# Two attention layers with heads of 16: projections ahead of the values, other banks for them, and a new order on ScalarE and VectorE

## The chip, the cores and the metric

The kernel runs on one core of a Trainium2 chip. Its engines are TensorE (PE; its weight loads are listed as PEld), VectorE (DVE), ScalarE (ACT), GpSimd (POOL) and SyncE (SP, which only issues transfers). The metric is the device time of one launch in microseconds; lower is better.

## The reference

The input x is 32 sequences of 64 tokens with 256 features, and ctx a second tensor of that shape. Four layers follow each other:

```python
x = L0(x, ctx, ctx)         # two cross attentions with 16 heads of 128, each behind a layer norm, and an MLP
x = L1(ctx, x, mask1)       # keys and values from concat(ctx, x): 128 keys, 16 heads of 16; norm, MLP
x = L2(x, ctx, mask2)       # layer norm, keys and values from ctx: 64 keys, 16 heads of 16; norm, MLP
x = L3(x, ctx)              # a 32-channel non-local block with a batch norm
```

The change touches L1 and L2, in their attention:

```python
q = (x_in @ q_w + q_b).reshape(B, Q, 16, 16)
k = (keys_in @ k_w + k_b).reshape(B, T, 16, 16);  v = (keys_in @ v_w + v_b).reshape(B, T, 16, 16)
weights = softmax(mask(einsum('bqhd,bthd->bhqt', q, k) * scale))
out = einsum('bhqt,bthd->bqhd', weights, v).reshape(B, Q, 256) @ out_w + out_b + residual
```

Q is 64; T is 128 in L1 and 64 in L2. All is computed in fp32; matrix products with weights run as three products of split operands (a high part rounded to the fast format, and the rest, the low part).

## The kernel before

`narrow` (L1215) builds both layers; `own` is true for layer 1. A layer is NU turns: 32 of one sequence in layer 1, 16 of two sequences in layer 2. NH = 8 half chunks of 256 tokens are projected, one for 4 turns in layer 1 (a group) and one for 2 in layer 2. A turn u covers all 16 heads, so its probabilities are 128 rows by 1024. Each engine has its program written out by hand, with semaphores between them:

- **TensorE** (`pe`, L1453): scores of u (`pe_scores`, L1410 for the mask and L1417), values of u - 3 (`pe_values`, L1447), the uses of banks of turn u (`pe_use`), transposes of u - 2 (`pe_transpose`, L1432).
- **ScalarE** (`act`, L1529): high part of the values of u - 3 (`act_hi`, L1579), the first use, the exponential (L1542), other uses whose bank the transposes need, the copy of the transposed probabilities of u - 2 (`act_probs`, L1565), the rest, and the normalised tiles of the next norm (L458).
- **VectorE** (`dve`, L1628): maximum (L1643) and subtraction (L1647) of u, low part of the values of u - 3 (`dve_lo`, L1618), its uses (`dve_use`: output unit L1612, bias row L1608), parts of a norm (statistics L384 and L409, rsqrt steps L433 to L442, a low half L488), sum (L1623) and reciprocal (L1626) of u - 1.
- **GpSimd** (`pool`, L1730): copies of keys (L1710), bias rows (L345), splits of weights (L1693, L1697), the power in a norm (L499), and the multiplication by the reciprocal (`pool_normalise`, L1755) of u - 1.

A use of a bank is a unit of matmuls that fills one of the 8 banks of the accumulator, and its eviction. Kinds: `q`, `kc`, `kh` (queries, keys from ctx, keys from x; evicted by ScalarE in L1503 and L1521), `v` (values; L1515), `norm` (transposes of a norm, L519; evicted by ScalarE in L533, with a high part in L537), `out` (output projection) and `row` (the bias row), both evicted by VectorE. `Slots.put` lists the uses of each turn in order, `bank_for` gives each its bank, and the unit waits until the use before it in that bank has been evicted. The projections all go through the helper `split3` (L175).

Banks: scores 0 to 3; transposes BT = 4 and 5; values BP = 6 in layer 1, 5 and 6 in layer 2; uses BJ, which share a bank with the transposes. A unit in bank 4 or 5 waits for the copy of the transposes that stood there, and the transposes wait for its eviction. In layer 2 the second half of the transposes (bank 5) also waits for the low part of the values that stood there (L1429).

## Time and profile before

| | |
|---|---|
| median of 3 runs | 1619.66 us (1619.57 to 1622.58) |
| the profiled execution | 1622.66 us |
| its span | 1621.1 us |
| TensorE busy | 1534.3 us, 95% |
| VectorE, ScalarE, GpSimd busy | 976.7, 861.7, 389.2 us |
| granted TensorE clock, mean | 0.993 |
| layer 1's attention | about 1038 to 1205 us |
| layer 2's attention | about 1311 to 1427 us |

The profile is of one execution. The span is from the first to the last instruction. Starts are counted from the start of the span; a line is that of the kernel, and for operations through a helper that of the helper. Engines overlap, so busy times do not add up to the span. A bracket behind a row tells how long its engine had been idle, and whose end released it.

### The profile page before, as it was taken

The numbers are of one execution on the slowest core, as the hardware profiler recorded it, in microseconds if no ns is written. First come the engines' busy times: TensorE is split into PE (matmuls) and PEld (weight loads), VectorE is DVE, ScalarE is ACT, GpSimd is POOL, SyncE is SP. The second block draws the span as 40 slices with busy tenths as digits, with TensorE's granted clock in tenths as the row PEclk, the third lists the DMA queues.
The fourth block names the chain that finished last, engine by engine and source line by source line (L and its number), as shares of the span: only waits on it lengthen the run. The fifth ranks groups of instructions, "written<-read, shape, count | busy, mean of one in ns | idle before, by whom it ended". The sixth has DMA issues, their size and how long they took to land. (4 is left out here: it accounts for less than half of the span.)

```text
span 1621.1 us, 43103 instructions
## 1 busy us (share of the span) xinstructions
PE 1534.3 (95%) x18156; PEld 1352.6 (83%) x18156; DVE 976.7 (60%) x2019; ACT 861.7 (53%) x1623; POOL 389.2 (24%) x365
## 2 busy tenths in 40 slices
PE   8999999999999999999999999888889987899995
PEld 6989888899888989988889889777778876788863
DVE  7755555555686555555555673588875565764366
ACT  5544444444455444444444555666776565665475
POOL 1211011101233110110111140166561133431042
PEclk9999999999999999999999999999999999999998
DMA  5111010000001101010100000200010000000001
GB/s 202 34 34 34 2 34 34 17 19 34 34 2 34 34 1 34 34 34 2 34 28 4 25 27 1 79 2 2 28 54 27 1 28 28 3 2 27 14 15 52
DMA packets 18701, 46.13 MB, mean 28 GB/s; under 512 B 1456, under 2 KB 11712, under 8 KB 15440
## 3 DMA queue, kind: packets, MB, share of 16 engines
q1 hardware_dynamic: 14320, 39.17, 7.1%
q10 hardware_dynamic: 4192, 4.24, 0.8%
q8 instruction: 144, 2.36, 0.6%
q14 instruction: 45, 0.37, 0.1%
HBM read 39.21 MB, written 4.19 MB: 27 GB/s over the span
## 5 line engine op out<-in xcount | busy, mean ns | idle before, releaser
L175 PE MATMUL ps<-ch,W 128*128 128x512 f32 (+1 forms) x2592 | 595.8, 377 | 4.5 <-DVE W L243 2.9
L175 PEld LDWEIGHTS ps<-ch,W 128*128 128x128 f32 x2592 | 439.4, 188 | 85.5 <-DVE W L243 3.2
L175 PEld LDWEIGHTS ps<-W,split_arena 128*128 128x128 f32 x3084 | 392.9, 189 | 41.3 <-issue 7.0
L175 PE MATMUL ps<-W,split_arena 128*128 128x256 f32 x3084 | 409.3, 284 | 16.5 <-DVE split_arena L1047 7.4
L175 PE MATMUL ps<-W,ch 128*128 128x256 f32 x1632 | 223.8, 287 | 0.0
L175 PEld LDWEIGHTS ps<-W,ch 128*128 128x128 f32 x1632 | 203.8, 191 | 1.0 <-ACT arena L776 0.2
L742 ACT ACTIVATE arena<-ps 64x256 f32<-64x256 f32 x256 | 97.0, 379 | 193.2 <-PE ps L655 190.1
L833 DVE TENSOR_REDUCE small<-ps 128x4 f32<-128x260 f32 x128 | 54.0, 422 | 204.0 <-PE ps L617 204.0
L791 ACT ACTIVATE arena<-ps,hbias 128x512 f32<-128x512 f32 x128 | 88.1, 688 | 126.7 <-PE ps L175 126.7
L210 POOL TENSOR_TENSOR arena<-arena 128x256 f32<-128x256 f32 x16 | 11.9, 742 | 588.0 <-PE ps L175 586.4
L916 DVE TENSOR_TENSOR arena<-ps,arena 128x512 f32<-128x512 f32 x128 | 88.0, 691 | 106.8 <-PE ps L175 105.6
L1047 DVE TENSOR_TENSOR split_arena<-arena,split_arena 128x512 fp32r<-128x512 f32 x96 | 70.2, 731 | 130.7 <-ACT split_arena L1079 121.6
L1755 POOL TENSOR_TENSOR arena<-arena,small 128x1024 f32<-128x1024 f32 x48 | 91.8, 1914 | 174.8 <-DVE small L1626 174.8
L765 ACT ACTIVATE arena<-arena 128x260 f32<-128x260 f32 x128 | 54.4, 425 | 139.5 <-DVE arena L836 139.5
L1076 ACT ACTIVATE arena<-ps,cols 128x512 f32<-128x512 f32 x96 | 66.0, 688 | 99.0 <-PE ps L175 97.3
L826 DVE SCALAR_TENSOR_TENSOR split_arena<-ps,hbias,split_arena 128x256 fp32r<-128x256 f32 x256 | 105.6, 474 | 1.5 <-ACT split_arena L749 1.5
L856 DVE TENSOR_TENSOR x_sb<-ps,x_sb 128x512 f32<-128x512 f32 x128 | 87.5, 687 | 18.2 <-PE ps L175 18.1
L749 ACT ACTIVATE split_arena<-ps,hbias 128x512 fp32r<-128x512 f32 x128 | 81.0, 684 | 26.1 <-PE ps L668 26.1
L668 PEld LDWEIGHTS ps<-arena 64*64 64x64 f32 x4096 | 65.5, 134 | 22.3 <-issue 21.8
L776 ACT ACTIVATE arena<-ps,hbias 128x512 f32<-128x512 f32 x128 | 80.1, 676 | 2.8 <-PE ps L175 2.8
L1643 DVE TENSOR_REDUCE small<-ps 128x8 f32<-128x1024 f32 (+1 forms) x48 | 58.2, 1212 | 34.7 <-PE ps L1417 34.2
L499 POOL TENSOR_TENSOR small<-small 128x4 f32<-128x4 f32 x24 | 26.5, 1103 | 218.2 <-DVE small L418 201.6
(135 smaller groups left out, 1972.5 us busy)
## 6 DMA issues: line engine op xcount, KB each, us to landing
raw<-wpack SPq DMA_DIRECT2D x23, 1028.0 KB, 5.0
arena<-vb_in SPq DMA_DIRECT2D x16, 256.0 KB, 5.1
x_sb<-x_in SPq DMA_DIRECT2D x4, 512.0 KB, 8.2
arena<-ctxT SPq DMA_DIRECT2D x4, 512.0 KB, 9.1
spill<-x_sb ACTq DMA_DIRECT2D x1, 2048.0 KB, 8.8
arena<-spill ACTq DMA_DIRECT2D x1, 2048.0 KB, 8.3
arena<-ctx_tok SPq DMA_DIRECT2D x16, 128.0 KB, 2.1
out<-x_sb SPq DMA_DIRECT2D x7, 256.0 KB, 2.5
```

Source lines behind the costliest of these rows:

```text
L175: last = e.matmul(dst, lhs[a], rhs[b], start=start and n == 0, stop=stop and n == 2, skip_group_check=True)
L668: ins = e.matmul(ps[dims, BO + b, at:at + SEQ], vs[t % 2][keys, n, h * DH0 + d * SEQ:h * DH0 + (d + 1) * SEQ], pts[h][keys, n, :], start=T ...
L742: ins = e.activation(pts[h][b * SEQ:(b + 1) * SEQ], own[:, :, b * SEQ:(b + 1) * SEQ], ACT.Copy)
L749: e.activation(head_split(h, 0), head_cells(h), ACT.Identity, bias=head_col(t, 3, h)).then_inc(a_oh, 1)
L776: e.activation(ks[h][:, :, key_slots(h)], cut(ps[:, h, :], BPC), ACT.Identity, bias=head_col(u, 1, h)).then_inc(a_ke, 1)
L791: e.activation(qs[h], ps[:, 2 + h, :], ACT.Identity, bias=head_col(u, 0, h)).then_inc(a_qe, 1)
L826: ins = e.scalar_tensor_tensor(head_split(h, 1)[:, :, b, :], head_cells(h)[:, :, b, :], head_col(t, 3, h), head_split(h, 0)[:, :, b, :].bi ...
L856: e.tensor_tensor(xs, cut(ps[:, banks[j], :], 2), xs, ALU.add).then_inc(a_acc, 1)
L916: e.tensor_tensor(vs[u % 2][:, 2 * j:2 * j + 2, :], cut(ps[:, j, :], 2), each(vdiff[u // NCH % 2], 2), ALU.add).then_inc(a_ve, 1)
L1047: e.tensor_tensor(gsp[f % 2][1], gelu[:, f % 2, :], gsp[f % 2][0].bitcast(F32), ALU.subtract).then_inc(s["gl"].sem, 1)
L1076: e.activation(gelu[:, f % 2, :], ps[:, f % 2, :], func, bias=col(f"fb{which}", f)).then_inc(s["gel"].sem, 1)
L1755: e.tensor_tensor(cells, cells, many(inv[w % 2], nk), ALU.mult).then_inc(nrm_done, 1)
```

## The change

Five edits, all in `narrow`:

1. Layer 1's uses alternate between banks 7 and 5, not 5 and 7, so that the first use of a turn has bank 7. The output unit comes last in its turn (before, it stood ahead of the keys from x, or of the values).
2. Layer 2 lists the keys (`kc`) first and the queries (`q`) last, behind the output unit. The bank is 4 for `row`, `norm` and the output unit of an even turn, else 7. Before, `kc` and `norm` had 4, the others 7.
3. TensorE issues the first `n_ahead` uses of a turn between the scores and the values: 3 in layer 1 (all of them), 1 in layer 2.
4. ScalarE evicts these uses ahead of the high part, and in layer 1 all evictions come ahead of the exponential. The high part of a norm's tile moves behind the copy of the probabilities (`act_norm_hi`).
5. VectorE computes the low part of the values behind the sum in layer 1, and in layer 2 behind the uses and the parts of a norm (before, right behind the subtraction).

Lines behind the edits move by 3 to 10: L1410, L1417, L1432, L1447 become L1413, L1420, L1435, L1450; L1503, L1515, L1521, L1542, L1565, L1579 become L1510, L1522, L1528, L1551, L1572, L1586; L1612, L1618, L1623, L1643, L1647 become L1620, L1626, L1631, L1651, L1655.

TensorE, layer 1, first two turns of the third group (turns 8 and 9), before. L1410 and L1417 are scores, L1447 values, L175 projections, L1432 transposes:

```order
L1410 MATMUL ps<-rows,small 128x2x64 x4
L1417 MATMUL ps<-arena 128x128 x8
L1447 MATMUL ps<-arena 32x64 x16
L175 MATMUL ps<-ch,W 128x256 x24
L1432 MATMUL ps<-cols,arena 128x128 x8
L1410 MATMUL ps<-rows,small 128x2x64 x4
L1417 MATMUL ps<-arena 128x128 x8
L1447 MATMUL ps<-arena 32x64 x16
L175 MATMUL ps<-W,split_arena 128x256 x6
L175 MATMUL ps<-ch,W 128x256 x12
L1432 MATMUL ps<-cols,arena 128x128 x8
```

and now:

```order
L1413 MATMUL ps<-rows,small 128x2x64 x4
L1420 MATMUL ps<-arena 128x128 x8
L175 MATMUL ps<-ch,W 128x256 x24
L1450 MATMUL ps<-arena 32x64 x16
L1435 MATMUL ps<-cols,arena 128x128 x8
L1413 MATMUL ps<-rows,small 128x2x64 x4
L1420 MATMUL ps<-arena 128x128 x8
L175 MATMUL ps<-ch,W 128x256 x12
L175 MATMUL ps<-W,split_arena 128x256 x6
L1450 MATMUL ps<-arena 32x64 x16
L1435 MATMUL ps<-cols,arena 128x128 x8
```

The queries and keys (24), and in the next turn the keys from x (12) and the output unit (6), moved ahead of the values.

ScalarE, layer 1, the first two turns of a group, before. L1579 is the high part, L1503 queries, L1521 keys, L1542 the exponential, L1565 the copy:

```order
L1579 ACTIVATE split_arena<-ps 128x2x64
L1503 ACTIVATE arena<-ps,small,cols 128x4x64 x4
L1542 ACTIVATE arena<-arena 128x1024
L1565 ACTIVATE arena<-ps 128x1024
L1521 ACTIVATE arena<-ps,cols 128x4x64 x2
L1579 ACTIVATE split_arena<-ps 128x2x64
L1542 ACTIVATE arena<-arena 128x1024
L1565 ACTIVATE arena<-ps 128x1024
L1521 ACTIVATE arena<-ps,cols 128x4x64 x2
```

and now:

```order
L1510 ACTIVATE arena<-ps,small,cols 128x4x64 x4
L1528 ACTIVATE arena<-ps,cols 128x4x64 x2
L1586 ACTIVATE split_arena<-ps 128x2x64
L1551 ACTIVATE arena<-arena 128x1024
L1572 ACTIVATE arena<-ps 128x1024
L1528 ACTIVATE arena<-ps,cols 128x4x64 x2
L1586 ACTIVATE split_arena<-ps 128x2x64
L1551 ACTIVATE arena<-arena 128x1024
L1572 ACTIVATE arena<-ps 128x1024
```

Both evictions of the first turn moved ahead of the exponential, and the high part behind them.

TensorE, layer 2, turn 10 (an even turn), before:

```order
L1410 MATMUL ps<-rows,small 128x256 x4
L1417 MATMUL ps<-arena 128x64 x16
L1447 MATMUL ps<-arena 32x64 x32
L175 MATMUL ps<-ch,W 128x256 x24
L175 MATMUL ps<-W,split_arena 128x256 x6
L1432 MATMUL ps<-cols,arena 128x128 x8
```

and now:

```order
L1413 MATMUL ps<-rows,small 128x256 x4
L1420 MATMUL ps<-arena 128x64 x16
L175 MATMUL ps<-ch,W 128x256 x12
L1450 MATMUL ps<-arena 32x64 x32
L175 MATMUL ps<-W,split_arena 128x256 x6
L175 MATMUL ps<-ch,W 128x256 x12
L1435 MATMUL ps<-cols,arena 128x128 x8
```

The keys (12 of the 24) stand ahead of the values, the queries (12) behind the output unit (6), just ahead of the transposes.

VectorE, layer 2, turn 12, before. L1618 is the low part, L1612 the output unit, L488 and L384 belong to norms:

```order
L1643 TENSOR_REDUCE small<-ps 128x16
L1647 TENSOR_TENSOR arena<-ps,small 128x1024
L1618 TENSOR_TENSOR split_arena<-ps,split_arena 128x2x2x64
L1612 TENSOR_TENSOR x_sb<-ps,x_sb 128x256
L488 TENSOR_TENSOR ch<-norm_arena,ch 128x512
L384 BN_STATS small<-x_sb 128x6 x4
L1623 TENSOR_REDUCE small<-arena 128x16
```

and now:

```order
L1651 TENSOR_REDUCE small<-ps 128x16
L1655 TENSOR_TENSOR arena<-ps,small 128x1024
L1620 TENSOR_TENSOR x_sb<-ps,x_sb 128x256
L488 TENSOR_TENSOR ch<-norm_arena,ch 128x512
L384 BN_STATS small<-x_sb 128x6 x4
L1626 TENSOR_TENSOR split_arena<-ps,split_arena 128x2x2x64
L1631 TENSOR_REDUCE small<-arena 128x16
```

The low part moved from behind the subtraction to behind the norm's parts.

```diff
--- before.py
+++ after.py
@@ -1230,7 +1230,7 @@
             wb = W[pack % 2]
             nth_pack, nth_pool = next(FAST), next(POOLED)
             scale = 1.0 / (DH1 if own else math.sqrt(DH1))
-            BT, BP, BJ = (4, 5), (6,) if own else (5, 6), (5, 7) if own else (7, 4)
+            BT, BP, BJ = (4, 5), (6,) if own else (5, 6), (7, 5) if own else (7, 4)
             S_done, T_done, P_done, J_in, A_out, V_out, kv_done = (
                 semaphore(f"h{layer}_{n}") for n in "scores probsT values filled act_out dve_out keysvalues".split())
             max_done, sub_done, exp_done, sum_done, inv_done, nrm_done, p_copied, hi_done, lo_done, x_bias, sel_done, b_split, v_zero = (
@@ -1280,6 +1280,8 @@
                 plan(nxt, 0, (8, 8, 9, 10, 12, 14), 9, (10, 10), (11, 13))
                 plan(nxt, 1, (12, 12, 13, 14, NU + 5, NU + 6), 13, (14, 15), (NU + 3, NU + 4))
             mid = 2 if own else 1
+
+            n_ahead = 3 if own else 1
             slots = Slots()
             slots.put(-1, ("q", 0), ("kc", 0), *([("kh", 0)] if own else []))
             for u in range(NU):
@@ -1289,23 +1291,24 @@
                 if own:
                     if r == 0 and more:
                         slots.put(u, ("q", nh), ("kc", nh))
-                    if r % 2 and u >= 5:
-                        slots.put(u, ("out", (u - 5) // 2))
                     if r == 1 and more:
                         slots.put(u, ("kh", nh))
                     if r >= 2:
                         slots.put(u, ("v", h, r - 2))
-                else:
-                    if r == 0 and more:
-                        slots.put(u, ("q", nh), ("kc", nh))
-                    if r == 1:
-                        slots.put(u, ("v", h, 0))
+                    if r % 2 and u >= 5:
+                        slots.put(u, ("out", (u - 5) // 2))
+                elif r == 0 and more:
+                    slots.put(u, ("kc", nh))
+                elif r == 1:
+                    slots.put(u, ("v", h, 0))
                 if u in turns:
                     slots.put(u, ("norm", *turns[u]))
                 if u == 0:
                     slots.put(u, ("row",))
                 if not own and u >= 4:
                     slots.put(u, ("out", u - 4))
+                if not own and r == 0 and more:
+                    slots.put(u, ("q", nh))
             for u in (NU + 3, NU + 4):
                 slots.put(u, ("norm", *turns[u]))
             last_outs = {NU + 1: 14, NU + 4: 15} if own else {NU: 12, NU + 2: 13, NU + 3: 14, NU + 4: 15}
@@ -1315,7 +1318,7 @@
             def bank_for(u, i, use):
                 if u >= NU:
                     return BT[use[3]] if use[0] == "norm" else 7 if own or u in (NU, NU + 4) else BT[1]
-                return BJ[i % 2] if own else BJ[use[0] in ("kc", "norm")]
+                return BJ[i % 2] if own else BJ[use[0] in ("row", "norm") or use[0] == "out" and u % UH == 0]
 
             slots.count((7, 5, 4) if own else (7, 4), bank_for, NU + 5)
             number = slots.number
@@ -1456,9 +1459,11 @@
                     pe_use(e, -1, use)
                 for u in range(NU):
                     pe_scores(e, u)
+                    for use in uses_of[u][:n_ahead]:
+                        pe_use(e, u, use)
                     if u >= 3:
                         pe_values(e, u - 3)
-                    for use in uses_of[u]:
+                    for use in uses_of[u][n_ahead:]:
                         pe_use(e, u, use)
                     if u >= 2:
                         pe_transpose(e, u - 2)
@@ -1483,11 +1488,13 @@
                         e.sem_inc(w_used.sem, 1)
                 return run
 
+            def act_norm_hi(e, use):
+                if use[0] == "norm":
+                    use[1].act_part(e, use[2], (slots.bank[use],) * KT, KT + use[3])
+
             def act_use(e, use):
                 if use[0] == "norm":
-                    b = (slots.bank[use],) * KT
-                    use[1].act_part(e, use[2], b, use[3])
-                    use[1].act_part(e, use[2], b, KT + use[3])
+                    use[1].act_part(e, use[2], (slots.bank[use],) * KT, use[3])
                 if use[0] not in slots.ON_ACT:
                     return
                 h, bank = use[1], bank_of(use)
@@ -1534,20 +1541,20 @@
                     e.wait_ge(before.sem, before.at(NCH - 1))
                     e.dma_start(spill.rearrange("(t p) d -> p t d", p=P), x_sb).then_inc(s_spill, 16)
                 for u in range(NU):
+                    for use in uses_of[u][:n_ahead]:
+                        act_use(e, use)
                     if u >= 3:
                         act_hi(e, u - 3)
-                    for use in uses_of[u][:1]:
+                    for use in uses_of[u][n_ahead:2]:
                         act_use(e, use)
                     e.wait_ge(sub_done, u + 1)
                     e.activation(t[u % 3], t[u % 3], ACT.Exp, scale=scale).then_inc(exp_done, 1)
-                    ahead = [use for use in uses_of[u][1:] if slots.bank[use] in BT]
-                    for use in ahead:
+                    for use in uses_of[u][max(2, n_ahead):]:
                         act_use(e, use)
                     if u >= 2:
                         act_probs(e, u - 2)
-                    for use in uses_of[u][1:]:
-                        if use not in ahead:
-                            act_use(e, use)
+                    for use in uses_of[u]:
+                        act_norm_hi(e, use)
                     for n, c, half in act_parts.get(u, ()):
                         if n is norm and n.kind == "none":
                             e.wait_ge(before.sem, before.at(NCH - 1))
@@ -1594,6 +1601,7 @@
                         act_hi(e, NU - 1)
                     for use in uses_of[NU + f - 1] if f >= 4 else ():
                         act_use(e, use)
+                        act_norm_hi(e, use)
                     if f == 5:
                         e.wait_ge(J_in, n_uses)
                         piece_act(e, pack + 2, nth_pack, 3)
@@ -1646,14 +1654,16 @@
                     m4 = mx[u % 2].rearrange("p j (g a) -> p j g a", a=1).to_broadcast([P, G // KT, NS, nk])
                     e.tensor_tensor(t[u % 3].rearrange("p (j k) (b n) -> p j (k b) n", k=KT, n=nk), cells, m4,
                                     ALU.subtract).then_inc(sub_done, 1)
-                    if u >= 3:
-                        dve_lo(e, u - 3)
                     for use in uses_of[u]:
                         dve_use(e, use)
                     for part in dve_parts.get(u, ()):
                         dve_norm(e, *part)
+                    if u >= 3 and not own:
+                        dve_lo(e, u - 3)
                     if u:
                         dve_sum(e, u - 1)
+                    if u >= 3 and own:
+                        dve_lo(e, u - 3)
                     if u == NU - 1:
                         piece_dve(e, pack + 2, nth_pack, 0)
                 dve_sum(e, NU - 1)
```

## Rows read from the trace of the kernel before

**Rows 1.** Page, part 1: engine, busy us (share of the span), instructions.

```profile
PE 1534.3 (95%) x18156; PEld 1352.6 (83%) x18156; DVE 976.7 (60%) x2019; ACT 861.7 (53%) x1623; POOL 389.2 (24%) x365
```

**Rows 2.** Windows: stretch, length, each engine's busy us (instructions), PEclk, DMA share, GB/s.

```profile
1038.00:1205.00 167.00, 145.57 (x2378) 127.38 (x2378) 143.38 (x221) 118.80 (x212) 95.45 (x83) 1.00 0.08 26
...
1079.04:1100.05 21.01, 18.61 (x318) 16.34 (x312) 16.56 (x23) 13.61 (x24) 13.19 (x13) 1.00 0.01 2
...
1100.05:1121.07 21.02, 18.61 (x319) 16.34 (x312) 19.08 (x37) 13.61 (x24) 12.41 (x12) 1.00 0.01 2
...
1184.00:1205.00 21.00, 16.53 (x256) 13.61 (x244) 20.45 (x40) 14.09 (x25) 11.88 (x10) 1.00 0.11 29
...
1326.00:1329.00 3.00, 1.71 (x8) 1.57 (x8) 1.77 (x5) 1.15 (x3) 1.05 (x1) 0.64 0.00 0
```

**Rows 3.** Waits, 1030 to 1230 us: who waited for whom, total us, times, longest.

```profile
PE ps L1447 <- ACT arena L1565: 14.7, 29, 0.9
```

**Rows 4.** Order of time on TensorE, layer 1, two turns: start, duration, engine, line.

```profile
1077.28 0.23 PE L1410 MATMUL ps<-rows,small 4*128 4x128 bf16 x4
...
1078.45 0.65 PE L1447 MATMUL ps<-arena 128*32 128x64 f32 x32 [0.44 <-ACT arena L1565]
...
1079.04 3.12 PE L175 MATMUL ps<-ch,W 128*128 128x256 f32 x24
...
1082.00 1.40 PE L1432 MATMUL ps<-cols,arena 128*128 128x128 f32 x8
...
1092.62 0.66 PE L1432 MATMUL ps<-cols,arena 128*128 128x128 f32 x4 [0.31 <-ACT arena L1515]
```

**Rows 5.** Order of time, layer 1, first turns of a group, ScalarE.

```profile
1101.78 1.93 ACT L1503 ACTIVATE arena<-ps,small,cols 128x256 f32<-128x256 f32 x4 [1.32 <-PE ps L175]
...
1103.60 1.06 ACT L1542 ACTIVATE arena<-arena 128x1024 f32<-128x1024 f32 x1
...
1104.55 1.03 ACT L1565 ACTIVATE arena<-ps 128x1024 f32<-128x1024 f32 x1
...
1105.45 0.86 ACT L1521 ACTIVATE arena<-ps,cols 128x256 f32<-128x256 f32 x2
...
1106.35 0.28 ACT L1579 ACTIVATE split_arena<-ps 128x128 fp32r<-128x128 f32 x1
```

**Rows 6.** Order of time, VectorE: layer 1, then layer 2.

```profile
1105.17 1.22 DVE L1643 TENSOR_REDUCE small<-ps 128x8 f32<-128x1024 f32 x1 [1.38 <-PE ps L1417]
...
1407.64 0.68 DVE L488 TENSOR_TENSOR ch<-norm_arena,ch 128x512 fp32r<-128x512 f32 x1
...
1408.24 1.40 DVE L384 BATCH_NORM_STATS2 small<-x_sb 128x6 f32<-128x256 f32 x4
```

**Rows 7.** Order of time, TensorE, layer 2, turns 10 and 11.

```profile
1385.01 0.29 PE L1410 MATMUL ps<-rows,small 4*128 4x256 bf16 x4
...
1390.70 0.97 PE L175 MATMUL ps<-W,split_arena 128*128 128x256 f32 x6 [0.59 <-ACT arena L1503]
...
1392.47 1.07 PE L1432 MATMUL ps<-cols,arena 128*128 128x128 f32 x8 [0.79 <-ACT arena L1521]
...
1393.47 0.29 PE L1410 MATMUL ps<-rows,small 4*128 4x256 bf16 x4
...
1400.59 0.29 PE L1410 MATMUL ps<-rows,small 4*128 4x256 bf16 x4
```

**Rows 8.** Order of time, layer 2, turn 14, TensorE.

```profile
1416.29 0.29 PE L1410 MATMUL ps<-rows,small 4*128 4x256 bf16 x4
...
1420.36 0.66 PE L1432 MATMUL ps<-cols,arena 128*128 128x128 f32 x4 [0.69 <-DVE split_arena L1618]
```

**Rows 9.** Order of time, layer 2, turns 2 and 3, TensorE.

```profile
1320.73 0.29 PE L1410 MATMUL ps<-rows,small 4*128 4x256 bf16 x4 [1.62 <-DVE arena L1647]
...
1327.29 1.94 PE L1432 MATMUL ps<-cols,arena 128*128 128x128 f32 x8 [2.36 <-ACT arena L1521]
```

## The prediction

> **What bounds the kernel now.** I read the page first, then the waits of TensorE in the stretches that the diff touches, then the order of time there. The page gives TensorE 95% busy over the span [rows 1]; that alone would leave little to win. But a busy TensorE in this view includes pipelined ends, and the two layers with heads of 16 are not average: from 1038 to 1205 us, layer 1, it is busy 145.57 of 167.00 us [rows 2]; layer 2 runs from 1311 to 1427 us. No transfer matters in layer 1 (DMA share 0.08 [rows 2]). The reader is to see that the missing time lies between TensorE's own instructions, turn after turn, and that each piece names ScalarE as its releaser.
>
> A turn is scores, values of three turns before, projections, transposes of two turns before. In layer 1 the values (L1447) stand right behind the scores and wait for ScalarE to copy the transposed probabilities (L1565), 14.7 us in 29 waits [rows 3]. Four turns (one half chunk, a group below) take 21.01 us: the second of the stretches, from the queries of one group to those of the next [rows 2]. Inside: waits of 0.44, 0.53, 0.44 and 0.53 us ahead of the values (the first stands in [rows 4], the pattern repeats), 0.31 us in the transposes at 1092.62, released by L1515, and 0.37 us hidden in the transposes at 1082.00, which take 1.40 us with queries and keys in the turn and 1.03 without. That is 2.62 us. Back-to-back work also starts before the modelled end of what is ahead (1079.04 against 1078.45 + 0.65 = 1079.10; 1082.00 against 1079.04 + 3.12 = 1082.16 [rows 4]); about 0.08 us each, so six vanished waits return another 0.5 us. Without any wait a group would be 21.01 - 2.62 - 0.5 = 17.9 us.
>
> VectorE is the second bound: 16.56 us busy in a group without normalisation work, 19.08 with the statistics of one chunk, 20.45 in the last [rows 2]. It has small gaps between dependent instructions; I add 0.6 us in a group of 21, so 17.2, 19.7 and about 20.4 (the last includes them in part).
>
> **Layer 1.** The edit puts up to three uses of banks between scores and values. They are at least 1.5 us of matmuls (a values projection is half of the 3.12 us at 1079.04 [rows 4]), more than the 0.53 us wait, so the four waits ahead of the values go. The swap of banks puts a lone values projection in bank 7; the 0.31 us wait goes, because the transposes need banks 4 and 5 only. What is late next: in the first turn of a group the keys now sit in bank 5. Counting from the turn's start, queries are filled at 0.67 + 1.49 = 2.16 us; ScalarE starts about 0.25 us later, takes 1.93 for queries and 0.86 for keys [rows 5]: 5.2 us. TensorE, after scores (1078.45 - 0.44 - 1077.28, less an overlap: 0.67), projections (1082.00 - 1079.04 = 2.96), values (1079.04 - 1078.45 = 0.58 with rounding) [rows 4] and the half of the transposes in bank 4 (0.48), stands there at 4.7. A new wait of 0.55 us replaces the hidden 0.37. A group: 17.9 + 0.55 = 18.45 us, and 18.9 where a normalisation's transposes (0.45) are in it; they were there before as well and stood where the 0.31 us wait was.
>
> ScalarE now empties before its exponential. In that first turn the exponential ends at 5.2 + 0.3 (L1579) + 1.06 = 6.6 us [rows 5], 0.8 us into the next turn. Its reader on VectorE, the sum, stands behind that turn's maximum and subtraction, which end 0.7 + 2 x 1.22 = 3.2 us into it (both are as long as the row of L1643 [rows 6]), so it costs nothing; 2.4 us is the margin. The copy of the probabilities ends 1.8 us into the next turn, where TensorE is still in its projections: nothing either. VectorE's low part behind the sum is free in layer 1: values need it a turn later.
>
> Against 21.0 now, the seven groups after the first: three with normalisation transposes and light VectorE, 3 x 2.1 = 6.3; one without, 2.55; one with statistics, VectorE 19.7 with some slack from its neighbours, 19.4: 1.6; one with statistics and low parts, about 20.1: 0.9; the last, bound by VectorE already (20.45 busy), 0.3. The first group waits for VectorE and GpSimd; only its fourth turn gains, 1.1. Sum **12.8 us**.
>
> **Layer 2.** Here an even turn has queries and keys, the output unit and the transposes. Turn 10 goes from 1385.01 to 1393.47, 8.46 us: waits of 0.59 (the output unit's bank, emptied by L1503) and 0.79 us (the transposes' bank 4, keys emptied behind the exponential), with their overlaps 1.72 [rows 7]. Now keys go to bank 7 before the values, the output unit to bank 4, queries last. Keys are emptied at 2.67 + 0.25 + 0.84 = 3.8 us, before queries start at 4.27; queries end at 5.76, and VectorE has added the output by 4.95. Both waits go: 6.75 to 6.9 us, so 1.55 saved. But VectorE's low part (0.41 us) now stands behind the output and the normalisation parts, and the transposes' bank 5 needs it. In turns 8 and 12 these parts are a low half and statistics, 0.68 + 1.40 us [rows 6]: 4.95 + 2.1 + 0.5 = 7.4 us against 6.25 wanted. I keep 0.75 and 0.5 us there. Turns 4 and 6 give 2.25 (another 0.67 wait ahead of the values) and 1.7. Even turns 4 to 12: 6.75.
>
> An odd turn with normalisation transposes (turn 11: 1393.47 to 1400.59, 7.12 us [rows 7], with two short waits for ScalarE) becomes 6.45: the 5.78 us that its instructions take back to back, plus some 0.2 for the eviction and 0.45 for the low part, which follows the output unit by 0.25 + 0.42 + 0.5 us where only 0.5 us of transposes covers it. Turns 5, 7, 11, 13: 2.25 together. Turns 9 and 15 have no such transposes and lose 0.5 and 0.1. Turn 14 has no queries to cover anything: now 4.66 us from 1416.29 to the end of the transposes at 1420.36, with a wait of 0.69 for the low part [rows 8]; then the output fills bank 4, VectorE reaches it at 3.7 (scores 1.18, then 2 x 1.23), and adds output 0.42, rsqrt steps 0.95, a low half 0.68 and the low part 0.41: 6.2, and the second half of the transposes ends the turn at 6.7: -2.05. Turns 4 to 15: 6.75 + 2.25 - 0.6 - 2.05 = 6.35.
>
> Turns 0 to 3: the bias row is filled before the queries, so VectorE's chain starts about 1.1 us sooner (the wait of 1.62 at 1320.73 [rows 9]). In turn 2 the transposes wait 2.36 us for bank 4 at 1327.29 [rows 9]; now no projection is in it, and instead the queries wait 1.0 us for the keys' bank: 1.36. And the granted clock there is 0.64 on average (between the levels 2.4 and 1.2 GHz [rows 2]): eight transposes take 1.94 us against 1.07 [rows 9, 7]. With the waits gone I expect the full level, about 2.7 us over the next 7. New waits for the low part take 0.7 off. Start: 4.45. Layer 2: **10.8 us**.
>
> The Trainium skill ("TensorE: Matmul & The Clock Gate", Part 1) says that the gate halves the clock after TensorE has been little busy and opens it with activity. By that rule the denser order keeps the clock and the sum stands; were it to fall all the same, the sum is 20.9 us in place of 23.6.
>
> **Sum.** 1622.66 (profiled execution) - 12.8 - 10.8 = 1599.1. The median shown is 3.0 us lower than that execution, about what the lowered clock costs; if most executions do not have it, their gain is smaller by as much and they end at the same place. Predicted: **1599**.
>
> **Rivals.**
> - *VectorE closes layer 1.* For: 19.08 of 21.02 us [rows 2], and four turns of different length with a fixed chain. Then each of seven groups saves 0.9, 6.3 us, layer 2 as forecast: 1622.7 - 6.3 - 10.8 = 1605.6. Against: groups without statistics need only 17.2. 14%.
> - *The low part behind the output closes layer 2.* Each even turn waits as turns 8 and 12 do: 5 us less, 1604. 10%.
> - *Slower: ScalarE's exponential behind the emptied banks closes the loop.* It decides from the point where an exponential ends later than VectorE's next subtraction, a margin of 2.4 us above. Then in the first turn of a group queries, keys, high part, exponential and copy run in series: 0.67 + 1.73 + 1.93 + 0.86 + 0.28 + 1.06 + 1.03 = 7.6 us [rows 5] against 6.1 now (0.67 scores, 0.44 wait, 0.58 values, 2.96 projections and 1.40 transposes [rows 4]), +1.4 in each of seven; in layer 2 9.0 against 8.46, +0.5 in each of five: 1622.7 + 12.6 = 1635. For: the queue is full of waits; against: ScalarE is busy only 118.80 of 167 us [rows 2]. 5%. The skill's same page (Part 1, architectural detail) says that ScalarE and VectorE run strictly in order; that is what this rival rests on.
> - *No effect:* the vanished waits come back whole behind bank 5 and VectorE: 1620. 4%.
>
> **Numbers.** Forecast 67%. About 0.2% (3.2 us) is what a measurement here can tell from no change. Faster 0.90, same 0.04, slower 0.06. Low end: with none of the new waits in either layer some 9 us more go, 1590; I take 1591. High end: both partial rivals together, 1611, and a little: 1613.
>
> **What would show it.** After: no wait of L1450 for L1572 in layer 1; a new wait of about 0.5 us inside one transpose pair in four, released by ScalarE's keys; groups of 18.4 to 18.9 us, 19.4 to 20.1 with statistics; in layer 2 even turns near 6.9 us, turn 14 longer than before, waits of L1435 on L1626, granted clock 1.00 at its start. Wrong: groups of 19.7 throughout (VectorE), or TensorE waiting long for L1572 again.

## The result, and the profile after

The change takes the median from 1619.62 us (4 runs) to 1602.09 us (4 runs, 1601.73 to 1602.56): ratio 0.9885, 95% interval 0.9873 to 0.9896. The forecast was 1599.0 (1591 to 1613), faster. The profiled execution after took 1601.73 us against 1622.66 before: 20.9 us less, where the medians differ by 17.5. What most likely makes the 3.4 us between them is told with layer 1 alone.

The page's part 1 of the kernel after, to be held against [rows 1]: TensorE does the same 18156 instructions in a span of 1600.1 us.

```profile
PE 1536.9 (96%) x18156; PEld 1354.5 (85%) x18156; DVE 977.0 (61%) x2019; ACT 859.9 (54%) x1623; POOL 389.9 (24%) x365
```

Windows after (stretch, length, busy us of PE, PEld, DVE, ACT, POOL, then clock, DMA share, GB/s): layer 1's attention, its second and third groups, its last, and 5 us of layer 2's last turn.

```profile
1038.00:1195.44 157.44, 148.91 (x2378) 128.87 (x2378) 142.15 (x221) 119.11 (x214) 96.43 (x84) 0.99 0.09 30
1055.25:1074.57 19.32, 19.17 (x317) 16.80 (x318) 17.43 (x24) 14.49 (x27) 13.49 (x11) 1.00 0.01 3
1074.57:1093.42 18.85, 18.70 (x313) 16.41 (x313) 16.95 (x23) 13.34 (x25) 12.59 (x12) 1.00 0.01 3
...
1171.59:1190.59 19.00, 16.25 (x281) 13.73 (x281) 18.11 (x33) 11.95 (x20) 10.84 (x9) 0.91 0.01 3
...
1398.00:1403.00 5.00, 5.00 (x57) 4.54 (x64) 2.85 (x4) 2.52 (x4) 3.28 (x3) 0.50 0.02 3
```

A group of four turns that took 21.0 us [rows 2] takes 18.85 or 19.32, and TensorE is without work for 0.15 us of it; the groups with statistics take 19.7. The last group is different: 2.75 us without work, and a clock of 0.91. At the end of layer 2 the clock stands at its lower level (0.50, 1.2 GHz).

TensorE's waits after, layer 1 (1038 to 1195 us). The 14.7 us of [rows 3], now L1450 for L1572, are down to one wait:

```profile
PE ps L1435 <- POOL arena L1765: 2.5, 3, 1.0
...
PE ps L1450 <- ACT arena L1572: 0.6, 1, 0.6
...
PE ps L1435 <- ACT arena L1528: 0.2, 1, 0.2
```

Order of time on TensorE after, the first turn of the third group and the start of its second, against [rows 4]:

```profile
1074.57 0.24 PE L1413 MATMUL ps<-rows,small 4*128 4x128 bf16 x4
1074.64 0.67 PE L1420 MATMUL ps<-arena 32*128 32x128 f32 x16
1075.24 3.13 PE L175 MATMUL ps<-ch,W 128*128 128x256 f32 x24
1078.30 0.65 PE L1450 MATMUL ps<-arena 128*32 128x64 f32 x32
1078.89 0.66 PE L1435 MATMUL ps<-cols,arena 128*128 128x128 f32 x4
1079.69 0.66 PE L1435 MATMUL ps<-cols,arena 128*128 128x128 f32 x4
1080.28 0.23 PE L1413 MATMUL ps<-rows,small 4*128 4x128 bf16 x4
```

The values follow the projections with no wait. Between the starts of the two halves of the transposes 0.80 us pass, where the prediction had 0.48: here the keys' eviction in bank 5 is waited for. The pair takes 1.39 us, 1.03 in other turns, so this new wait costs 0.36.

In layer 2 TensorE's waits (1290 to 1410 us) now name VectorE's low part:

```profile
PE ps L1435 <- DVE split_arena L1626: 6.0, 7, 1.5
...
PE ps L1435 <- DVE x_sb L1620: 1.2, 1, 1.2
```

Where it comes from is seen in turn 12: output (L1620), a low half and statistics stand ahead of the low part, first VectorE, then TensorE:

```profile
1380.40 0.43 DVE L1620 TENSOR_TENSOR x_sb<-ps,x_sb 128x256 f32<-128x256 f32 x1 [0.80 <-PE ps L175]
1380.75 1.26 DVE L488 TENSOR_TENSOR ch<-norm_arena,ch 128x512 fp32r<-128x512 f32 x1
1381.93 1.39 DVE L384 BATCH_NORM_STATS2 small<-x_sb 128x6 f32<-128x256 f32 x4
1383.24 0.40 DVE L1626 TENSOR_TENSOR split_arena<-ps,split_arena 128x256 fp32r<-128x256 f32 x1
```
```profile
1381.64 0.60 PE L1435 MATMUL ps<-cols,arena 128*128 128x128 f32 x4
1383.69 0.55 PE L1435 MATMUL ps<-cols,arena 128*128 128x128 f32 x3 [1.45 <-DVE split_arena L1626]
```

The waits for the low part stand in turns 3, 8, 9, 12, 13, 14 and 15. Turn 14 has two waits, and behind them the clock is at its lower level, 0.50 over the last turn's first 5 us:

```profile
1395.33 0.63 PE L1435 MATMUL ps<-cols,arena 128*128 128x128 f32 x4 [1.20 <-DVE x_sb L1620]
1397.08 1.11 PE L1435 MATMUL ps<-cols,arena 128*128 128x128 f32 x4 [1.12 <-DVE split_arena L1626]
```

### The profile page after: what moved, and what is told of

Its sections match the earlier page's. It is cut to its first block and busy times, and to the rows that moved or that the text cites. A ratio compares the mean times of both kernels' runs of the same rounds, so it can differ in the third digit from the quotient of the medians.

```text
span 1600.1 us, 43100 instructions
## 1 busy us (share of the span) xinstructions
PE 1536.9 (96%) x18156; PEld 1354.5 (85%) x18156; DVE 977.0 (61%) x2019; ACT 859.9 (54%) x1623; POOL 389.9 (24%) x365
## 5 line engine op out<-in xcount | busy, mean ns | idle before, releaser
L175 PE MATMUL ps<-ch,W 128*128 128x512 f32 (+1 forms) x2592 | 597.8, 377 | 5.2 <-DVE W L243 2.3
L175 PEld LDWEIGHTS ps<-ch,W 128*128 128x128 f32 x2592 | 439.9, 188 | 87.3 <-issue 3.0
L175 PEld LDWEIGHTS ps<-W,split_arena 128*128 128x128 f32 x3084 | 393.3, 189 | 32.8 <-issue 6.7
L175 PE MATMUL ps<-W,split_arena 128*128 128x256 f32 x3084 | 408.5, 284 | 10.2 <-DVE split_arena L1047 7.4
L175 PE MATMUL ps<-W,ch 128*128 128x256 f32 x1632 | 224.4, 287 | 1.2 <-ACT arena L1510 1.0
L175 PEld LDWEIGHTS ps<-W,ch 128*128 128x128 f32 x1632 | 204.3, 191 | 2.4 <-ACT arena L1510 1.9
L228 POOL TENSOR_TENSOR W<-raw,W 128x512 fp32r<-128x512 f32 x60 | 75.7, 1297 | 1.2
```

The costliest lines, as they stand in the source:

```text
L175: last = e.matmul(dst, lhs[a], rhs[b], start=start and n == 0, stop=stop and n == 2, skip_group_check=True)
L228: ins = e.tensor_tensor(W[b][1][:, a], raw[:, a], W[b][0][:, a].bitcast(F32), ALU.subtract)
```

## The experiments

Twelve kernels, one of them the change again, in three batches, each batch on one chip with the kernel before (median there 1622.13, 1622.27 and 1620.64 us, spread 1618.1 to 1627.1). Differences to the change are against its 1602.09 us, in the third batch against its 1601.80 there. The executions of one changed kernel lie 0.8 to 5.3 us apart, so a difference of 2 us between batches is no result by itself. Diffs are against the changed kernel, those of `l1_only` and `l2_only` cut to the lines that tell the choice.

| kernel | median us | lowest to highest | ratio to before, 95% interval |
|---|---|---|---|
| l1_only | 1608.33 | 1606.99 to 1612.27 | 0.9916, 0.9900 to 0.9932 |
| l2_only | 1611.49 | 1609.21 to 1613.52 | 0.9934, 0.9918 to 0.9950 |
| lo_first2 | 1593.81 | 1592.20 to 1593.95 | 0.9818, 0.9802 to 0.9834 |
| sum_first1 | 1611.55 | 1608.42 to 1612.68 | 0.9931, 0.9916 to 0.9947 |
| act_back1 | 1650.11 | 1646.95 to 1650.80 | 1.0177, 1.0160 to 1.0194 |
| banks_back1 | 1618.05 | 1616.98 to 1620.96 | 0.9976, 0.9965 to 0.9986 |
| lo_first1 | 1610.43 | 1607.84 to 1612.77 | 0.9929, 0.9911 to 0.9947 |
| q_first2 | 1607.65 | 1607.33 to 1609.03 | 0.9916, 0.9899 to 0.9932 |
| after_again | 1601.80 | 1600.74 to 1602.55 | 0.9879, 0.9859 to 0.9899 |
| bank14 | 1592.16 | 1590.54 to 1592.66 | 0.9817, 0.9800 to 0.9835 |
| sum_first1b | 1600.58 | 1599.63 to 1602.29 | 0.9876, 0.9856 to 0.9897 |
| combo | 1591.99 | 1590.33 to 1593.64 | 0.9821, 0.9803 to 0.9838 |

**Each layer alone.** First layer 1 alone, then layer 2 alone; the banks and TensorE's, ScalarE's and VectorE's order in the other layer are those of before.

```diff
-            n_ahead = 3 if own else 1
+            n_ahead = 3 if own else 0
```
```diff
-            BT, BP, BJ = (4, 5), (6,) if own else (5, 6), (7, 5) if own else (7, 4)
+            BT, BP, BJ = (4, 5), (6,) if own else (5, 6), (5, 7) if own else (7, 4)
...
-            n_ahead = 3 if own else 1
+            n_ahead = 0 if own else 1
```

> Layer 1 as in the change, layer 2 entirely as before (its queries ahead of the keys, its banks, its low part behind the subtraction, ScalarE's order). If the two layers' gains are separate and the traces' own lengths hold (layer 1 10.1 us between its first turn and the next layer's transposes), the time is 1619.6 - 10.1 = 1609.5 us (1608.3 to 1611). Rival, the forecast's own split (layer 1 12.8): 1606.8. Rival, that layer 1 brings little by itself and layer 2 most of the gain: 1614 or more.

> Layer 2 as in the change, layer 1 entirely as before. By the two traces layer 2 gave 10.5 us (3.4 in its turns 0 to 3, 7.1 in turns 4 to 15), of which the lowered clock at its start in the trace of before is about 3. If the median runs of before don't have that lowered clock, the time is 1619.6 - 7.5 = 1612.1 us (1610.8 to 1613.2); if they have it, 1609.1. With l1_only the two gains should sum to 17.5 us; a sum over 20 or under 15 would mean that the layers act on each other, over the clock for one.

Layer 1 alone: 1608.33, between the two theories' 1609.5 and 1606.8. Both were counted from 1619.6, though; against the 1622.13 of the kernel before in this batch the gain is 13.8 us, above both. From layer 1's first scores to layer 2's first is 261.4 us in its trace, 261.9 with both layers changed, 272.5 before: the layer's gain is its own. Layer 2 alone: 1611.49, the case of a median without those 3 us; but its runs stand in two heaps, 1609.2 to 1610.6 and 1612.4 to 1613.5. The two gains (13.8 and 10.6 us) sum to more than the 20.0 of both (1622.13 to 1602.1). In the profiled execution of layer 2 alone the clock stayed at 1.00 through the last turns, and from turn 0 to the end of the span it is 2.7 us shorter than with both. That is a size for the excess. The two waits ahead of the last turn are the same as with both, and the row of the window is the last turn's first 5 us:

```profile
1406.68 0.63 PE L1435 MATMUL ps<-cols,arena 128*128 128x128 f32 x4 [1.20 <-DVE x_sb L1630]
1408.44 0.66 PE L1435 MATMUL ps<-cols,arena 128*128 128x128 f32 x4 [1.12 <-DVE split_arena L1636]
```
```profile
1409.03:1414.03 5.00, 4.91 (x123) 4.35 (x122) 3.66 (x6) 4.51 (x8) 3.29 (x3) 1.00 0.02 3
```

So these waits alone don't decide whether the clock falls; what does stays open.

Layer 1 alone also bears on the 3 us by which the profiled execution of before lies above its median. It runs layer 2 as before, and has turns 5 to 8 of 7.13, 8.44, 7.12 and 8.45 us where the profiled execution of before has 7.61, 9.37, 7.97 and 9.45. That one has this group of waits in 1330 to 1380 us, and these rows in turn 6, a values step cut in two. The view counts 2.3 us as idle; the four turns are 3.3 us longer:

```profile
PE ps L1447 <- issue: 2.3, 4, 0.8
```
```profile
1353.20 0.79 PE L1447 MATMUL ps<-arena 64*32 64x64 f32 x57
1354.67 0.31 PE L1447 MATMUL ps<-arena 64*32 64x64 f32 x7 [0.68 <-issue]
```

Turns 2 and 3, with the lowered clock that the forecast spoke of, have 0.89 and 0.61 in layer 1 alone and 0.86 and 0.64 before, and turn 2 takes 8.40 and 8.43 us: that clock is in both. That the median executions of before have no such stalls is likely by this, but only one of them was profiled.

**Low part of layer 2 first again.**

```diff
+                    if u >= 3 and not own:
+                        dve_lo(e, u - 3)
                     for use in uses_of[u]:
                         dve_use(e, use)
                     for part in dve_parts.get(u, ()):
                         dve_norm(e, *part)
-                    if u >= 3 and not own:
-                        dve_lo(e, u - 3)
```

> The change, but layer 2's low part stands right behind VectorE's subtraction again, ahead of the projections' uses; all else as in the change. Theory A: TensorE's waits for the low part in layer 2 (0.81, 0.88, 0.90, 1.45, 0.46, 1.12, 0.41: 5.6 us in six of them in the stretch 1290 to 1405) come from the place that the change gave it behind the uses; they go, and the lowered clock at the layer's end, behind the last of them, with them (about 2 us): 1602.1 - 5.6 - 1.9 = 1594.6 us, 1594 to 1598. Theory B: the low part isn't ready to be made earlier, since ScalarE's high part ends about 4.2 us into the turn, and VectorE waits for it with the uses queued behind: the waits move to the projections' transposes and the gain is under 2 us, or a loss (1600 to 1604).

Theory A, 0.8 us below its figure and just under its range. The waits for the low part in layer 2:

```profile
PE ps L1435 <- DVE split_arena L1626: 0.8, 1, 0.8
```

From turn 0 to turn 15 layer 2 is 6.0 us shorter (91.85 for 97.86), from there to the end of the span 2.8, with the clock at 1.00 where the change has 0.50. The wait for the output in bank 4 of turn 14 stays (1.5 us). Of the 2.8 us the clock makes 2.3, by the trace of layer 2 alone, which has it at 1.00 without this edit; against that trace (297.2 us from turn 0 to the end of the span, here 291.1) the low part's place is worth 6.1 us.

**Turn 14's output in bank 7**, on top of the last.

```diff
-... else BJ[use[0] in ("row", "norm") or use[0] == "out" and u % UH == 0]
+... else BJ[use[0] in ("row", "norm") or use[0] == "out" and u % UH == 0 and u < NU - 2]
```

> Layer 2's low part right behind the subtraction (as in lo_first2, 1593.8 us), and turn 14's output unit in bank 7 in place of bank 4. Theory A: the wait of the transposes for that output (1.5 us, released by VectorE's L1620) goes, as no transposes stand in bank 7: turn 14 from 6.35 to 5 us, 1592.4 us. Theory B: the transposes then wait for the normalisation of the probabilities or the norm's own transposes instead, and under 0.5 us is left: 1593.3 to 1594.

In turn 14 theory A: it goes from 5.50 us (6.96 in the change) to 4.66, as long as before. In the time it is not shown. Turn 15 up to the matmuls behind its transposes takes 5.81 us for 5.11, because its transposes now wait for GpSimd's normalisation (first `bank14`, then `lo_first2`):

```profile
1395.81 1.34 PE L1435 MATMUL ps<-cols,arena 128*128 128x128 f32 x8 [0.24 <-POOL arena L1765]
```
```profile
1397.51 1.03 PE L1435 MATMUL ps<-cols,arena 128*128 128x128 f32 x8
```

From layer 2's first scores to the end of the span the two traces have 291.0 and 291.1 us. The 1.3 us between their profiled executions all lie ahead of layer 1, where the program is the same, and the 1.65 between the medians are between two batches.

**Queries first again in layer 2.**

```diff
-                    slots.put(u, ("kc", nh))
+                    slots.put(u, ("q", nh), ("kc", nh))
...
-                if not own and r == 0 and more:
-                    slots.put(u, ("q", nh))
...
-... else BJ[use[0] in ("row", "norm") or use[0] == "out" and u % UH == 0]
+... else BJ[use[0] in ("kc", "norm")]
```

> The change, but layer 2 lists queries first, keys behind them, and has its banks of before (keys and norm 4, the others 7); one use still goes ahead of the values, now the queries. Theory A: the keys are filled about 5.0 us into an even turn and emptied at 6.1, where the transposes want bank 4 at 5.8 to 6.0: 0.3 more in each of six even turns, and the bias row comes behind the queries again (1.1 us at the start) and turn 2's wait for bank 4 comes back (up to 1.4): 1602.1 + 2 to 4.5 = 1604 to 1606.6 us. Theory B: the low part closes these turns anyway (5.6 us of waits), so that the keys' bank is hidden behind it: 1601.5 to 1603.

5.6 us slower than the change, more than theory A's end. Its even turns 4 to 12 take 7.31, 7.93, 9.22, 8.18 and 9.66 us against 6.68, 6.70, 7.79, 6.76 and 8.37, the odd ones behind them 6.28 to 6.47, up to 0.7 less. Turn 13 takes 9.30 us for 6.87, at a clock of 0.69 behind turn 12's wait of 1.81 us, which neither theory had. The keys' bank cost the 0.3 us that was expected, but the output unit came later too, and the low part behind it: 9.5 us of waits for it, not 6.0.

```profile
PE ps L1433 <- DVE split_arena L1624: 9.5, 9, 2.5
PE ps L1433 <- ACT arena L1526: 3.0, 6, 1.4
```

**The swap of banks undone in layer 1.**

```diff
-            BT, BP, BJ = (4, 5), (6,) if own else (5, 6), (7, 5) if own else (7, 4)
+            BT, BP, BJ = (4, 5), (6,) if own else (5, 6), (5, 7) if own else (7, 4)
```

> The change, but layer 1's uses start with bank 5 again. In a group's first turn the keys then have bank 7 and the queries bank 5: the wait of the transposes for the keys goes (forecast 0.55, the trace shows 0.15 and a longer pair of transposes), so that turn gets 0.2 to 0.5 shorter. In the third turn the lone values projection stands in bank 5: filled 2.3 us into the turn, emptied at 3.2, where the transposes want it at 3.3: 0 to 0.5 longer. Theory A: the two cancel, 1600.5 to 1603.5 us, and the swap was worth nothing. Theory B (the swap's reason in the forecast, a 0.31 us wait per group removed, and the transposes of a norm too): 2 to 4 us slower, 1604 to 1606.

Both theories fall: 16.0 us slower. One exchange of two digits holds more than the whole gain of layer 1. A unit in bank 5 may not start before ScalarE has copied the transposes that stood there, and with bank 5 first the unit behind the scores is that unit. Waits (1040 to 1205 us), and a turn's unit on TensorE with the copy on ScalarE ahead of it:

```profile
PE ps L175 <- issue: 15.1, 21, 1.1
PE ps L175 <- ACT arena L1572: 5.4, 6, 1.2
```
```profile
1106.46 1.06 ACT L1572 ACTIVATE arena<-ps 128x1024 f32<-128x1024 f32 x1
```
```profile
1107.62 1.66 PE L175 MATMUL ps<-ch,W 128*128 128x256 f32 x12 [1.11 <-issue]
```

The view names "issue" in 21 of 27, but here the copy ends at 1107.52, and the unit starts 0.10 behind it; at 1095.85 and 1101.12 it is the same to 0.01 us. So the wait for the copy that stood ahead of the values is back, ahead of the projections, 0.5 to 1.2 us each, and nothing covers it.

**ScalarE's order of before in layer 1.**

```diff
-                    for use in uses_of[u][:n_ahead]:
+                    old = own
+                    for use in () if old else uses_of[u][:n_ahead]:
                         act_use(e, use)
                     if u >= 3:
                         act_hi(e, u - 3)
-                    for use in uses_of[u][n_ahead:2]:
+                    for use in uses_of[u][:1] if old else uses_of[u][n_ahead:2]:
                         act_use(e, use)
+                        if old:
+                            act_norm_hi(e, use)
...
                     e.activation(t[u % 3], t[u % 3], ACT.Exp, scale=scale).then_inc(exp_done, 1)
```

> The change, but ScalarE in layer 1 has its order of before: high part, first use, exponential, the uses that the transposes' banks hold, copy, the rest. TensorE's order and the banks stay. Theory A (ScalarE's new order is what lets the projections stand ahead of the values): in a group's first turn the high part now waits for the values, which end about 4.2 us into the turn, then follow queries 1.93, exponential 1.06, keys 0.84, and the second half of the transposes waits for the keys in bank 5 until about 8.3 us: 8.8 us in place of 5.7, 3.1 more in each of seven or eight groups, 1602.1 + 22 to 25 = 1624 to 1627, slower than the kernel before. Theory B (TensorE's order alone gives the gain, ScalarE has slack): under 1606.

Theory A's mechanism at twice its price: 48.0 us slower than the change, outside its range. First turns of a group take 9.3 us (5.7 in the change); ScalarE holds queries and keys back behind the high part and the exponential, and TensorE stands 3.31 us:

```profile
1089.92 0.28 ACT L1596 ACTIVATE split_arena<-ps 128x128 fp32r<-128x128 f32 x1 [2.65 <-PE ps L1450]
1090.10 1.93 ACT L1510 ACTIVATE arena<-ps,small,cols 128x256 f32<-128x256 f32 x4
1091.89 1.07 ACT L1554 ACTIVATE arena<-arena 128x1024 f32<-128x1024 f32 x1
1092.84 0.86 ACT L1528 ACTIVATE arena<-ps,cols 128x256 f32<-128x256 f32 x2
```
```profile
1093.75 1.11 PE L1435 MATMUL ps<-cols,arena 128*128 128x128 f32 x4 [3.31 <-ACT arena L1528]
```

The expectation left out the other turns (a norm's evictions, L533, 11.0 us of waits in six) and the clock, 0.91 over 1040 to 1240 us.

**Low part of layer 1 first again**: the diff of `lo_first2`, with `own` for `not own`.

> The change, but in layer 1 VectorE makes the low part right behind the subtraction again. In a group's first turn ScalarE ends the high part 5.5 us in (behind queries and keys), VectorE is done with its subtraction at 3.2 and would wait 2.3 us with the sum queued behind. Theory A (VectorE is near its bound in the groups with statistics): each group loses 0.5 to 1.5 us, 1605.5 to 1612. Theory B (VectorE's slack of 2 us and more in a group takes it): within 1 us of the change, 1601 to 1603.

8.3 us slower than the change, in theory A's range, but not where it put it. VectorE does wait for ScalarE's high part, 14.0 us in 18; the first turn of a group keeps its 5.70 us all the same, while the second and fourth grow from 4.6 to 5.3: there the output's eviction in bank 5 is queued behind that wait.

```profile
1085.51 0.29 DVE L1626 TENSOR_TENSOR split_arena<-ps,split_arena 128x128 fp32r<-128x128 f32 x1 [0.46 <-ACT split_arena L1586]
1085.71 0.41 DVE L1620 TENSOR_TENSOR x_sb<-ps,x_sb 128x256 f32<-128x256 f32 x1
```
```profile
1086.18 0.66 PE L1435 MATMUL ps<-cols,arena 128*128 128x128 f32 x4 [0.47 <-DVE x_sb L1620]
```

**VectorE's sum ahead of the norm in layer 1**, in two forms.

```diff
+                    sum_first = own and all(part[1] != "var" for part in dve_parts.get(u, ()))
+                    if u and sum_first:
+                        dve_sum(e, u - 1)
                     for part in dve_parts.get(u, ()):
                         dve_norm(e, *part)
...
-                    if u:
+                    if u and not sum_first:
                         dve_sum(e, u - 1)
```

> The change, but in layer 1 VectorE makes a turn's row sum ahead of its norm steps (save in the turns with a variance step). Theory A: layer 1's gain fell short in the last group (1.04, 0.93 and 1.84 us of wait for GpSimd's normalisation, behind VectorE's sum, and a clock of 0.50 to 0.66 for some 4 us behind the first of them), and an earlier sum gives 1.5 to 3 us back: 1599 to 1600.6 us. Theory B: the shortfall lies mostly in the seams of the turns (0.1 to 0.15 us in each of 28), on which the sum has no bearing, and the waits for the normalisation pass to the norm's own chain: 1601.5 to 1602.5 us.

Neither: 9.5 us slower. The last group did get shorter (13.1 us for its first three turns against 14.1; 13.5 in the trace of `after_again`, where the clock did not fall). But VectorE's rsqrt steps of turn 23 now stand behind the sum and ScalarE's norm waits for them, with the next turn's evictions queued behind; the group behind turn 23, turns 24 to 27, takes 24.83 us for 19.31. In turn 31 it happens again (ScalarE waits 2.55 us), and layer 2 starts 3.9 us later for it.

```profile
1154.99 1.09 ACT L458 ACTIVATE norm_arena<-x_sb,cols,small 128x256 f32<-128x256 f32 x2 [3.27 <-DVE small L439]
```

The second form excepts the rsqrt turns as well: `part[1] not in ("var", "newton")`.

> The change, but in layer 1 VectorE makes the sum ahead of the norm steps, save in turns with a variance or an rsqrt step (in sum_first1 the rsqrt chain moved behind the sum held ScalarE for 3.27 us in turn 23 and 2.55 in turn 31, with evictions queued behind it). Theory A: the groups with statistics and the last group keep what sum_first1 showed there (0.23 us in each of two, 1.0 in the last group), and the two losses (5.5 and 3.9 us) don't come: 1602.1 - 1.5 = 1600.6 us. Theory B: other norm steps moved behind the sum (statistics, low halves) hold ScalarE or TensorE as the rsqrt did: 1602.5 us or more.

In the turns theory A: the two groups with statistics take 19.45 instead of 19.67, the last group's three turns 13.1 instead of 13.5. In the time a gain is not shown: 1600.58 is 1.2 us under the change on the same chip, but the executions (1599.63 to 1602.29, and 1600.74 to 1602.55) overlap, and from layer 1's first scores to layer 2's the traces have 261.1 and 261.5 us.

**The change again, and all three together.** `after_again` has no edit; `combo` has those of lo_first2, bank14 and sum_first1b.

> The change itself once more, beside the three below and the kernel before on the same chip. Theory A: the 3 us between the profiled execution of before and its median are the stalls of four values steps in layer 2 (0.20, 0.68, 0.62 and 0.76 us named issue, with 7.61, 9.37, 7.97 and 9.45 us for turns 5 to 8, where the kernel with layer 1 alone changed has 7.13, 8.44, 7.12 and 8.45), which come in some executions only, and a dip of the clock at 937 to 944 us that comes in some: then this kernel stays within 1600 to 1605 while the kernel before spreads from 1619.5 to 1626. Theory B: the chip's state moves both alike: this kernel spreads over 6 us as well.

> The edits of lo_first2, bank14 and sum_first1b together. If the three gains add (8.3, 1.4, 1.5 us on 1602.1) it is 1591 us, 1590 to 1592.5, the fastest of all; if the gains in layer 2 overlap (bank14 nothing) or the sum costs, 1592.5 to 1594.5.

The change spreads over 1.8 us where the kernel before spreads over 7.5: nearer to theory A, with 4 executions against 9. But the layers' own variants spread as well (5.3 us in `l1_only`, 4.9 in `lo_first1`), and for the cause only the one trace with stalls speaks: it is not shown. The combination is 1591.99, 9.8 us under the change and the same as bank14 (1592.16): the earlier sum adds nothing that these runs can show.

## Why the prediction was right, and where it was not

**Time and sign: right, the time in part by luck.** It is 3.1 us too low, well inside the range. By its own steps, profiled execution against profiled execution, it forecast 12.8 + 10.8 = 23.6 us and 20.9 came. But 3.3 of these are the stalls inside values steps, which were no term of the forecast: it took what turns 4 to 15 save from rows without stalls and left the stalls in its base of 1622.66. Its own terms brought 17.6 of 23.6 us: 10.6 of 12.8 in layer 1 (from its first scores to layer 2's), 7.2 of 10.8 in layer 2, less 0.15 by which layer 1 started later.

**Waits of the values (L1447) go: right.** 14.7 us to 0.6. But the reason given for the swap was wrong. The prediction put it down for a 0.31 us wait of a lone values projection, once in a group. `banks_back1` shows that without it the wait for the copy only moves, at 16.0 us. The rule was in the code as read (a unit in bank 4 or 5 waits for the copy that stood there); the forecast never applied it to the first unit's start. It had the right banks by the change, not by its reasoning.

**New wait in bank 5: right in place, smaller**: 0.36 us for 0.55.

**A group of 18.45 or 18.9 us: 18.85 or 19.32.** The step that failed is "six vanished waits return another 0.5 us". 21.01 - 2.62 + 0.36 is 18.75 already. The overlap behind the scores came (0.67 for 0.73 us), but from the start of the projections to what follows is 3.06 us now that values follow (1075.24 to 1078.30) and was 2.96 with transposes behind them [rows 4]. In the other three turns it is 2.33, 1.63 and 2.34 for 2.25, 1.54 and 2.26: 0.35 us in a group. A pair of transposes behind the values takes 1.03 us for 0.97. Together that eats the 0.5. The three groups with a norm's transposes gave 5.0 for 6.3, the one without 2.16 for 2.55.

**VectorE in groups with statistics: about right**, 1.34 and 1.33 for 1.6 and 0.9; its bound was set too high in the second. **The last group: right only where the clock holds.** 0.3 forecast; its first three turns lost 0.27 (14.12 us for 13.85), and 0.4 with the stretch up to layer 2's first scores. There turns have no queries to cover anything, TensorE waits for GpSimd's normalisation behind VectorE's sum, and the clock stands at 0.50 for 2 us behind the first such wait. In the trace of `after_again` that wait is as long (1.04 us), the clock stays at 1.00, and the three turns take 13.48, a gain of 0.37.

**Layer 2: right in sum (10.5 for 10.8), by two errors that cancel.** Turns 4 to 15 gave 7.1 for 6.35, but 3.3 of these are the stalls, seen only in the profiled execution of before (turns 5 to 8, against the trace of layer 1 alone). Without them these turns gave 3.8. The step that failed is the clock, which was forecast at its full level and fell at the layer's end. With it at 1.00, layer 2 alone against layer 1 alone, turns 4 to 15 take 81.9 us for 88.4: 6.5 us, as forecast. Turn 15 took 7.96 us where 6.1 was forecast and layer 2 alone has 5.73, turn 14 took 6.96 for 6.7 (6.51 there).

The low part's waits were foreseen well: turn 8 took 7.79 for 7.7, turn 12 8.37 for 7.95, turn 9 lost 0.2 for 0.5. What the forecast didn't price is the low part left in its old place: by `lo_first2` that is worth 8.3 us, 6.1 without the clock. The rival "the low part closes layer 2" (1604) had 5 us more of these waits, at every even turn; at 6.7 to 6.8 us turns 4, 6 and 10 have none. Turns 0 to 3: 3.4 for 4.45.

**The median note: wrong.** The 3.0 us by which the median of before lies below its profiled execution were put down to the lowered clock at layer 2's start. That is in the trace of layer 1 alone too, whose values steps have no stalls. So the gain from the median is 17.5 where the traces give 20.9. If the stalls explain the 3.0, all 23.6 us should have come off the median: 1619.66 - 23.6 = 1596, and 1602.09 is 6 us above that.

**The clock: half right.** It is 1.00 at layer 2's start. It now falls at the end of layer 2 and, for some us, in layer 1's last group, each time behind waits of about 1 us, but not in every execution that has these waits. By the Trainium skill ("TensorE: Matmul & The Clock Gate", Part 1) the gate falls after TensorE has been little busy; the traces agree with that for the place (1.20 and 1.12 us of waits in turn 14, then 0.50), and `l2_only` shows that it isn't the whole of it (the same waits, then 1.00). The forecast had looked for the clock only where the change removes waits.

**Rivals.** VectorE closing layer 1 did not happen: groups of 18.85 and 19.3, and 19.7 only where there are statistics. The slower rival, the exponential behind the evictions, did not either. The opposite was near: with the evictions behind the exponential the kernel is slower than before, 1650. No run has ScalarE's new order with TensorE's old one, or moves the output unit alone, so what these bring by themselves is not shown.

## What to carry to other kernels

Moving a unit ahead of a wait helps only if its own start is free of the same event: follow each of its semaphores, the one on its buffer among them, before counting the wait as gone. Edits that look like details of one move (a swap of banks, another engine's order) can be what makes it work: here undoing one costs 16 us and the other 48, where the layer gained 10.6. An instruction that is put late on an in-order engine because its reader has slack must be checked in each layer and turn: the same low part is worth 8.3 us behind the sum in layer 1 and costs 8.3 us behind the norm in layer 2. A difference of 1 to 2 us between medians of two batches should be looked for in the traces: the turn that got shorter in `bank14` gave its gain back in the next.

## What the runs showed of the hardware

- Four values steps of one execution stood still in the middle (0.20, 0.68, 0.62, 0.76 us, named "issue"), and turns 5 to 8 were 3.3 us longer; no other trace of this case shows a values step cut in two. What caused it was not tried.
- Ahead of layer 1 the program is the same in all kernels, and up to 931 us the 14 traces agree within 0.3 us. Yet the granted clock over 936 to 944 us was 1.00, 0.79 or 0.57, and layer 1's first scores stood at 1036.6 to 1036.8, 1038.0 to 1038.4 and 1039.1 to 1039.4 us accordingly: 2.8 us between executions from one dip.
- Behind the same waits the clock fell in one execution and not in another: 1.20 and 1.12 us in turn 14 of layer 2, then 0.50 in the change and 1.00 in `l2_only`; 1.04 us in layer 1's last group, then 0.50 for 2 us in the change and no fall in `after_again`.
